# Centring rows on TensorE: a bfloat16 product with turned means in place of a float32 product with a broadcast column

## What is computed

```python
h = maximum(layernorm(x), 0)                      # per row: (x - mean) / sqrt(var + eps)
msg = (h[src] @ W1 + h[src]*h[dst] @ W2) * (norm[src] * norm[dst])   # per edge
h_N = segment_sum(msg, dst) + h @ W1              # dense part: every row
y = where(h_N >= 0, h_N, 0.2*h_N)
out = x + y / maximum(sqrt(sum(y*y, axis=1)), 1e-12)
```

## Time and profile before

| | |
|---|---|
| median of 3 runs | 1258.09 us (1256.14 to 1296.67) |
| span of the profiled execution (first to last instruction) | 904.7 us |
| VectorE busy | 800.7 us (89%) |
| ScalarE busy | 780.3 us (86%) |
| TensorE busy (products / weight loads) | 724.0 / 701.2 us (80% / 78%) |
| GpSimd busy | 692.5 us (77%) |
| mean granted TensorE clock | 0.937 |

### The profile page before, as it was taken

How to read it: one execution, slowest core, us unless ns; L and a number is a source line. 1 busy time by engine, 2 the same in 40 slices (tenths; PEclk the granted TensorE clock), 3 DMA queues, 4 the chain that set the end, 5 groups by cost and what they waited for, 6 DMA issues and landing times.

```text
span 904.7 us, 21801 instructions
## 1 busy us (share of the span) xinstructions
PE 724.0 (80%) x6300; PEld 701.2 (78%) x6300; DVE 800.7 (89%) x2616; ACT 780.3 (86%) x3211; POOL 692.5 (77%) x694
## 2 busy tenths in 40 slices
PE   1399989888898897798798889878979887978930
PEld 1398878888887887798798788878978887878830
DVE  6778999999999989897898899788989888989991
ACT  0389999999999897899899899897998899979960
POOL 1777878878888878888888788788878878877643
PEclk9999999999999998999899999898998999989975
DMA  2912757566574675476466656645755665665532
GB/s 68 314 51 75 260 173 236 195 212 235 187 260 166 198 249 172 163 230 219 172 197 218 201 187 231 204 166 176 239 206 170 212 241 166 211 215 178 184 124 84
DMA packets 68938, 172.92 MB, mean 191 GB/s; under 512 B 14411, under 2 KB 34542, under 8 KB 62674
## 3 DMA queue, kind: packets, MB, share of 16 engines
q1 hardware_dynamic: 50002, 135.41, 44.3%
q0 software_dynamic: 18816, 36.08, 12.8%
HBM read 96.89 MB, written 77.04 MB: 192 GB/s over the span
## 4 chain that ended last, share of the span: by engine, by line
POOL 70%; issue 19%; DVE 4%; ACT 2%; DMA 1%; POOLq 1%; PE 1%; SPq 0%; DVEq 0%; ACTq 0%
POOL xd L487 23%; POOL xs L487 23%; POOL out L492 22%; POOL stage L498 2%; POOL sstage L503 1%; DVE xo L866 1%; DMA out<-oe,sstage 1%; ACT junk L1082 0%; DMA out<-xo 0%; ACT ybuf L1143 0%; DVE oe L855 0%; DVE bst L818 0%; DVE agg L910 0%; DVE ybuf L874 0%; SPq L334 0%
## 5 line engine op out<-in xcount | busy, mean ns | idle before, releaser
L1223 PE MATMUL pt<-ident,xin 128*128 128x128 f32 x784 | 233.5, 298 | 97.5 <-DVE bst L818 97.5
L1226 PE MATMUL pt<-nident,bst 128*128 128x128 f32 x1568 | 303.2, 296 | 0.0
L492 POOL DMA_INDIRECT out<-oe,sstage x196 | 244.9, 1250 | 53.9 <-issue 52.6
L1226 PEld LDWEIGHTS pt<-nident,bst 128*128 128x128 f32 x1568 | 268.0, 214 | 0.0
L487 POOL DMA_INDIRECT xs<-in_x,stage x196 | 213.9, 1091 | 53.3 <-issue 53.3
L487 POOL DMA_INDIRECT xd<-in_x,stage x196 | 206.0, 1051 | 59.8 <-issue 59.8
L1082 ACT ACTIVATE junk<-ybuf 128x128 bf16<-128x128 f32 x772 | 248.6, 474 | 0.0
L1236 PE MATMUL pu<-w,ct 128*128 128x128 f32 x1568 | 206.9, 280 | 17.8 <-ACT ct L1066 17.7
L1236 PEld LDWEIGHTS pu<-w,ct 128*128 128x128 f32 x1568 | 188.8, 193 | 22.5 <-ACT ct L1066 22.5
L1223 PEld LDWEIGHTS pt<-ident,xin 128*128 128x128 f32 x784 | 121.4, 155 | 108.3 <-issue 63.0
L1082 ACT ACTIVATION_READ_ACCUMULATOR junk<-ybuf 128x1 f32 x772 | 202.6, 335 | 0.0
(11 more groups left out here) (146 smaller groups left out, 1280.4 us busy)
## 6 DMA issues: line engine op xcount, KB each, us to landing
xin<-in_x SPq DMA_DIRECT2D x96, 512.0 KB, 4.1
out<-xo SPq DMA_DIRECT2D x48, 1024.0 KB
srow<-src_rows SPq DMA_DIRECT2D x49, 256.0 KB, 6.3
edge_rows<-oe SPq DMA_DIRECT2D x49, 256.0 KB
same<-same_segment SPq DMA_DIRECT2D x49, 128.0 KB
xs<-in_x,stage POOLq DMA_INDIRECT x196
xd<-in_x,stage POOLq DMA_INDIRECT x196, 2.6
out<-oe,sstage POOLq DMA_INDIRECT x196
```

The lines of the kernel that those rows point to most:

```text
L492: pool.indirect_dma_start(out=out, out_offset=bass.IndirectOffsetOnAxis(ap=index, axis=0), in_=rows, in_offset=None, bounds_check=row_limi ...
L1223: pe.matmul(pt[:, q % 2, f], xin[:, s.buf(), col * D:(col + 1) * D], ident[:], is_transpose=True, start=True, stop=False)
L1226: last = pe.matmul(pt[:, q % 2, f], mean[:, s.buf(0, 2), col:col + 1].to_broadcast([P, D]), nident[:], start=False, stop=True)
```

## The change

The mean of a row is split into three bfloat16 numbers that add up to it exactly: VectorE takes the upper half of the mean's 32 bits (read in place as bfloat16), writes the rest into the count's slot of `bst`, takes the upper half of that, and writes what is left into the slot of the sum of squares (which `stats_guard` has read by then). So `bst` holds 48 bfloat16 numbers (16 rows, three parts each) in a partition. TensorE turns them with one product a step (`turn_means`: 48 columns as weights, `nidb`, minus the identity in bfloat16, as the moving operand) into 48 partitions x 128 columns of the second half of `pt`, ScalarE copies that to `turned_mean` in SBUF as bfloat16, and then each row's centring is one bfloat16 product over 48 partitions: `pick` has ones at the three parts of that row. Neither DMAs nor their queues are touched.

```diff
-        nident = sb("nident", [P, P])
+        nidb = sb("nidb", [P, P], BF16)
+        pick = sb("pick", [P, TD], BF16)
+        turned_mean = sb("turned_mean", [3 * TD, P], BF16)
...
+        def mean_words(h):
+            return bst[:, h, 0:3 * TD].rearrange("p (t w) -> p w t", w=3)
+
+        def mean_tops(h):
+            return bst[:, h, 0:3 * TD].bitcast(BF16).rearrange("p (k u) -> p u k", u=2)[:, 1, :]
...
-            dve.tensor_scalar(nident[:], ident[:], -1.0, None, ALU.mult).then_inc(s_const, 1)
+            dve.tensor_scalar(nidb[:], ident[:], -1.0, None, ALU.mult)
+            with nc.allow_low_precision(reason="one of three terms is 1, the others 0"):
+                dve.tensor_reduce(pick[:], ident[:, 0:3 * TD].rearrange("p (t w) -> p t w", w=3), AX.X, ALU.add
+                                  ).then_inc(s_const, 1)
...
+            def mean_part(s, d, part):
+
+                h = s.buf(d, 2)
+                words, tops = mean_words(h), mean_tops(h).rearrange("p (t w) -> p w t", w=3)
+                if part == 0:
+                    dve.tensor_tensor(words[:, 0, :], words[:, 1, :], tops[:, 1, :], ALU.subtract).then_inc(part_done, 1)
+                else:
+                    dve.wait_ge(part_done, s(d + 1))
+                    dve.tensor_tensor(words[:, 2, :], words[:, 0, :], tops[:, 0, :], ALU.subtract).then_inc(parts_done, 1)
...
+            for part in range(2):
+                mean_part(Step(0, 0), 0, part)
...
                     if has(i, 1):
                         stats_guard(s, 1)
+                        mean_part(s, 1, 0)
                     if has(i, -2):
                         out_dense(s, 8, 9)
+                    if has(i, 1):
+                        mean_part(s, 1, 1)
...
                 if has(i, 0):
+                    act.wait_ge(mean_turned, s(1))
+                    act.copy(turned_mean[:], pt[0:3 * TD, 1, 0:P]).then_inc(mean_evac, 1)
                     relu_quarter(0)
...
-                        last = pe.matmul(pt[:, q % 2, f], mean[:, s.buf(0, 2), col:col + 1].to_broadcast([P, D]),
-                                         nident[:], start=False, stop=True)
+                        last = pe.matmul(pt[:, q % 2, f], pick[0:3 * TD, col:col + 1].to_broadcast([3 * TD, D]),
+                                         turned_mean[:], start=False, stop=True)
                     last.then_inc(t_done, 1)
+
+                def turn_means():
+                    pe.wait_ge(parts_done, s(1))
+                    pe.matmul(pt[0:3 * TD, 1, 0:P], mean_tops(s.buf(0, 2)), nidb[:], start=True, stop=True
+                              ).then_inc(mean_turned, 1)
+                    pe.wait_ge(mean_evac, s(1))
...
                 if has(i, 0):
-                    pe.wait_ge(bn_done, s(1))
+                    if has(i, -1):
+                        pe.wait_ge(t_evac, s() * NQ)
+                    turn_means()
                     turn_quarter(0)
```

More of the change, by code:

```diff
@@ L260, in gnn_preln_kernel @@
         bn_done = sem("bn_done")
+        part_done = sem("part_done")
+        parts_done = sem("parts_done")
+        mean_turned = sem("mean_turned")
+        mean_evac = sem("mean_evac")
         edge_bn_done = sem("edge_bn_done")
@@ L1220, in turn_quarter @@
                     for t in range(4):
-                        f = slice(t * D, (t + 1) * D)
-                        col = q * 4 + t
+                        col, f = q * 4 + t, slice(t * D, (t + 1) * D)
                         pe.matmul(pt[:, q % 2, f], xin[:, s.buf(), col * D:(col + 1) * D], ident[:],
                                   is_transpose=True, start=True, stop=False)
-                        last = pe.matmul(pt[:, q % 2, f], mean[:, s.buf(0, 2), col:col + 1].to_broadcast([P, D]),
-                                         nident[:], start=False, stop=True)
+                        last = pe.matmul(pt[:, q % 2, f], pick[0:3 * TD, col:col + 1].to_broadcast([3 * TD, D]),
+                                         turned_mean[:], start=False, stop=True)
                     last.then_inc(t_done, 1)
+                def turn_means():
[3 more added lines that the diff above has]
+                    pe.wait_ge(mean_evac, s(1))
                 def mul_quarter(q):
```

## The result

The changed kernel takes 1514.08 us (median of four runs, 1505.09 to 1518.85) against 1268.86 us for the kernel before in the runs beside it: a ratio of 1.201, 95% interval 1.193 to 1.209. The forecast was 1294 us with a range to 1314: the direction held, the size did not. The loss is 245 us where 36 were summed. A ratio given with an interval compares the runs of both kernels in their faster state alone; a ratio "by the medians" takes all runs.

A forecast was written before the change was run, and what follows sets the result against it. ScalarE with its round trip was to become the bound: 15.69 + 2.12 = 17.81 us a step against 17.04, over 45 steps +34.7, with start and end +36 us, so 1258 + 36 = 1294 us, range 1264 to 1314.

The forecast's parts named there:

- The base: Under the sum: a step of 17.04 us from VectorE's scan, with 353.4 us around the span left as is.
- The turn: On TensorE, transposing plus new centring product: 0.11 + 0.056 us at full clock, 0.21 + 0.107 at low clock.
- The round trip: From ScalarE's copy to its first clip: 1.51 us at full clock, 2.12 at low; 2.12 a step as priced.
- TensorE behind the copy: Hand-over from ScalarE's copy to TensorE takes 0.05 us; ScalarE's wait for the turned means is covered.
- The clock: TensorE's idle gap of some 4.8 us brings low clock to the first quarter of three steps in four.
- low clock throughout: Rival, chance 0.08: TensorE's work doubled exceeds a step; step 18.3 us and above, +58 us, 1316 us or more.
- The signs I named: Profile after: copy to clip 1.5 to 2.2 us, scatter waits almost gone, clips 17.6 to 18.1 apart, clock under 0.9.
- The sign of being wrong: Wrong if clips stay 17.5 us apart with scatter waits, clock stays 1.00, or a turn misses about 0.17 us.
- TensorE does not set the pace of before: TensorE waits for VectorE's statistics in both regimes; losing some 2.7 us of work a step alone gives nothing.

The follow-up runs named there:

- e4: Changed kernel with its centring products over 128 partitions in place of 48, the other 80 holding zeros, round trip kept: 1269.94 us, ratio 1.031.
- e6: Changed kernel with 128-partition products; ScalarE copies the turned means earlier and does three more sums of squares before its first clip: 1279.75 us, 0.995 by the medians.
- e1: The kernel before, unchanged, run again for its span and a second trace: 1260.01 us with a span of 1258.3 us.
- e9: Changed kernel with SyncE's plain loads of fixed rows in place of the gathers: 1222.76 us.
- e13: Against the kernel before: centring by three 16-bit products over 128 partitions, mean's parts used where they lie, nothing turned or copied: 1267.04 us, ratio 1.020.
- e14: Against the kernel before: centring by two 16-bit products with only the mean's two upper parts, nothing turned or copied: 1259.59 us, ratio 1.016.
- e5: Changed kernel with products over 128 partitions and no round trip, moving operand zeros so the mean stays on: 1252.05 us, ratio 0.966.

## Why the prediction was wrong, step by step

- **The base.** "What lies around the span (353.4 us, median less span) I leave as it is" failed. The sum was made against a step of 17.04 us that the timed runs do not have; theirs is 22.90, with TensorE's increments late while GpSimd issues indirect DMAs. The difference of time and span was the sign: 353 us is 28% of the time, and I put it where no view could contradict it.
- **The turn.** This is the term that carries the miss: "It is nearest to the second; by columns that is 0.056" was mis-sized for this form. The pair measured 0.42 us at full and 0.62 at low clock in place of 0.17 and 0.32; with 96 or 128 partitions it is 0.17 and 0.32. The rows I bounded it by were all of products over 128 partitions, so no bound covered the form that was added. Sixteen turns a step, each 0.25 to 0.30 us longer, are 4.0 to 4.8 us; from 128 to 48 partitions the step grew by 5.24 us (28.34 - 23.10) with gathers and by 5.43 (23.39 - 17.96) with plain loads, and from 96 to 64 by 4.72 (27.67 - 22.95). Beside a round trip that is most of the loss of 5.44 us a step; without the trip the same product costs 1.42. With the turn as it was priced the kernel takes 1269.94 us, 1.031 of before (e4): inside the forecast's range, though from a base that was not there, so that agreement is luck in part.
- **The round trip.** 1.51 to 2.12 us was right in its terms: 1.94 us on the mean where nothing else disturbs, 2.96 in the changed kernel, with the long turns as the difference (4 x 0.25 to 0.30 = 1.0 to 1.2 us). The sign that was named, 1.5 to 2.2 us from copy to clip, holds for 2 of the changed kernel's 49 steps and for 41 of 49 with 128 partitions (e4). The trip's worth depends on what it meets: 1.52 us a step with plain loads and short turns, 1.1 to 1.7 with gathers and short turns, 2.80 with the old product, 4.02 with the 48-partition one (28.34 - 24.32). So the time from copy to clip was right for the turn that it was summed with, and its worth of 2.12 was put some 0.4 to 1.0 us too high. Why a longer turn makes the trip dearer by more than its own four turns is argued in the next point and not shown.
- **TensorE behind the copy.** I priced the hand-over to TensorE at 0.05 us and called the wait for the turned means covered. In the changed kernel TensorE stands still 5.8 us a step on the mean between the product of the means and its first turn: the increment comes late, by 2.7 us on the mean, and ScalarE, which waited for late ones too, first finishes its step (2.8 us), then copies. In the order of before TensorE was free to turn two quarters in that time. No run takes this cost away by itself: e6 shortened the wait, and the time moved by no more than its spread.
- **The clock.** A low clock in three steps of four was the right direction, and too little: the mean is 0.709, against 0.814 in e1. Of the turns in the changed kernel's trace some four in five ran at the low clock, in e1 one in five. The rival "low clock throughout" (0.08, 1316 us or more) is the nearest to what came, by its time and by its bound: in e9 TensorE is 68% of the chain that ended last.
- **The signs I named.** ScalarE's wait before each first clip came, but longer than named. VectorE's scatter waits gone and a mean clock under 0.9 came too, and tell nothing, since e1 has both. First clips 17.6 to 18.1 us apart: only with 128 partitions and plain loads (a step of 17.96). TensorE 100 us less busy did not come (1044.8 us). The sign of being wrong, a turn that does not fall to about 0.17 us at full clock, did: 0.42.
- **TensorE does not set the pace of before.** e13 and e14 bear it out: they shorten the turns and gain nothing. e5 (0.966) leaves a doubt. Of the changed kernel it is otherwise: the prediction had ScalarE with its trip as the bound, and the chain that ended last is 40% TensorE and 28% ScalarE.

## What to carry to other kernels

Before costing anything, compare the span of the profile with the timed median: if they differ by more than a few us, the rows describe another execution, and its step is no base for a sum. A new form of product is priced by a row of that form, its number of partitions included; pad a short contraction to more than half of the partitions when it alternates with full ones (96 of 128 were enough here). An exchange between two engines in every step can cost more than its own terms: here 1.1 to 4.0 us, by what TensorE had left to do behind it.

## What the runs showed of the hardware

- A 16-bit product over 48 or 64 partitions in turn with a float32 one over 128: the pair takes 0.42 us at 2.4 GHz and 0.62 at 1.2; over 96 or 128 it takes 0.17 and 0.32. With 48 the load of its weights starts after 0.22 us of idle time (at 1030.64); with 128 it runs under the product before.
- In e1 TensorE's semaphore increments arrive late, by 4.3 us on the mean, while GpSimd issues rows of indirect DMAs, and on time outside (0.09 us); in the first profile of before they arrive on time throughout. Eight plain loads from SyncE in place of eight gathers took 31% off the time of the kernel before.
- In this kernel 2352 centring products of 16 bits in place of 784 float32 ones (1568 records) brought no gain (ratio 1.020, 1.006 to 1.035), though the turn was shorter (0.28 us against 0.34).
